# Conditional residual block on one core: LoRA factors and base in SyncE's queue, two packs mixed before the first LoRA product, 24 warm-up matmuls

## The reference

```python
masked_w = weight * mask[None]                                  # (8, 256, 256)
w_bot = einsum('bg,got->bot', cond, masked_w)                   # layer 0's weight per sample
x = x + einsum('bnt,bot->bno', x, w_bot) + bias0
out = einsum('btc,oc->bto', x, W_base) + b_base                 # layer 1's base
h = einsum('btc,erc->bter', x, As)
lora = einsum('bter,eor,be->bto', h, Bs, cond) * 2.0            # rank 16, 8 experts
x = x + out + lora
```

## Time and profile before

| what | us |
|---|---|
| median of 3 runs | 61.73 |
| lowest and highest of them | 61.02 and 61.81 |
| the profiled execution: its own time | 61.96 |
| the profiled execution: its span | 60.0 |

### The profile page before, as it was taken

The page is one execution under the profiler, slowest core; times in us unless marked ns, Lnnn a source line. Parts: engine busy times, 40 slices in busy tenths (PEclk is TensorE's granted clock), DMA queues, the critical chain, the costliest instruction groups (busy, mean ns, idle before and its releaser), DMA issues.

```text
span 60.0 us, 983 instructions
## 1 busy us (share of the span) xinstructions
PE 53.4 (89%) x335; PEld 48.4 (81%) x335; DVE 43.2 (72%) x65; ACT 31.3 (52%) x52; POOL 31.7 (53%) x29
## 2 busy tenths in 40 slices
PE   3926999999999789999978999999999999999910
PEld 3906999999999568898866889989988989888900
DVE  0001983798599699899999999999996974835030
ACT  0805934030760688900299999497099391340700
POOL 4000704403992009999049999999999991000000
PEclk9999999999999999999999999999999999999999
DMA  0889999999999930000026350543140532514472
GB/s 0 138 296 406 404 398 404 407 405 412 412 401 409 401 134 11 0 0 0 0 89 261 116 227 12 186 169 130 51 175 30 205 120 106 206 37 175 175 255 94
DMA packets 5332, 11.79 MB, mean 196 GB/s; under 512 B 592, under 2 KB 1104, under 8 KB 5328
## 3 DMA queue, kind: packets, MB, share of 16 engines
q1 hardware_dynamic: 5040, 11.21, 49.3%
q10 hardware_dynamic: 288, 0.53, 3.0%
HBM read 7.54 MB, written 4.19 MB: 196 GB/s over the span
## 4 chain that ended last, share of the span: by engine, by line
PE 56%; POOL 12%; DVE 9%; issue 9%; DMA 7%; ACT 2%; POOLq 0%; DVEq 0%
PE ps_out L484 9%; PE ps_out L444 9%; PE ps_out L446 9%; PE ps_out L450 9%; DMA packs_sb<-head_dram 7%; PE ps_merge L450 4%; POOL W_lo L195 4%; DVE W L328 4%; POOL W L199 4%; PE ps_merge L446 4%; PE ps_merge L444 4%; PE ps_lora L444 3%; PE ps_lora L446 3%; PE ps_lora L450 3%; POOL W_lo L189 2%
## 5 line engine op out<-in xcount | busy, mean ns | idle before, releaser
L339 DVE TENSOR_TENSOR x_lo<-x_sb,x_hi 128x1024 fp32r<-128x1024 f32 x8 | 12.2, 1530 | 0.0
L189 POOL TENSOR_TENSOR W_lo<-W,W_hi 128x512 fp32r<-128x512 f32 x8 | 10.9, 1359 | 2.4 <-ACT W_hi L232 2.4
L195 POOL TENSOR_TENSOR W_lo<-W,W_hi 128x512 fp32r<-128x512 f32 x6 | 10.1, 1691 | 2.3 <-ACT W_hi L238 2.3
L484 PE MATMUL ps_out<-packs_sb 128*128 128x128 f32 x64 | 9.8, 314 | 1.6 <-DMA packs_sb<-head_dram 1.6
L199 POOL TENSOR_TENSOR W<-W,ident 128x256 f32<-128x256 f32 x6 | 8.5, 1424 | 4.2 <-DVE x_lo L339 4.2
L484 PEld LDWEIGHTS ps_out<-packs_sb 128*128 128x128 f32 x64 | 9.2, 226 | 1.8 <-DMA packs_sb<-head_dram 1.8
L444 PE MATMUL ps_out<-x_hi,M_hi 128*128 128x512 f32 (+1 forms) x32 | 9.9, 390 | 0.3 <-DVE x_lo L339 0.3
L446 PE MATMUL ps_out<-x_lo,M_hi 128*128 128x512 f32 (+1 forms) x32 | 9.7, 384 | 0.0
L450 PE MATMUL ps_out<-x_hi,M_lo 128*128 128x512 f32 (+1 forms) x32 | 9.7, 384 | 0.0
L261 ACT ACTIVATE out_sb<-ps_out,bias_sb 128x512 f32<-128x512 f32 x8 | 5.5, 686 | 7.0 <-DVE bias_sb L419 4.2
L311 DVE SCALAR_TENSOR_TENSOR A_lo<-lora_sb,A_hi 128x256 fp32r<-128x256 f32 x8 | 5.0, 621 | 4.8 <-ACT A_hi L224 4.8
(11 more groups left out here) (49 smaller groups left out, 81.6 us busy)
## 6 DMA issues: line engine op xcount, KB each, us to landing
x_sb<-xT_dram SPq DMA_DIRECT2D x8, 512.0 KB, 10.8
outT_dram<-out_sb SPq DMA_DIRECT2D x15, 256.0 KB, 2.0
packs_sb<-packs_dram SPq DMA_DIRECT2D x7, 288.0 KB, 6.1
rows_sb<-rows_dram SPq DMA_DIRECT2D x1, 384.0 KB, 8.0
lora_sb<-lora_dram ACTq DMA_DIRECT2D x1, 262.0 KB, 4.4
base_sb<-base_dram ACTq DMA_DIRECT2D x1, 256.0 KB, 5.1
outT_dram<-out_sb SPq DMA_DIRECT2D x2, 128.0 KB, 1.8
packs_sb<-head_dram SPq DMA_DIRECT2D x1, 192.0 KB, 4.2
```

The lines of the kernel that those rows point to most:

```text
L189: pool.tensor_tensor(W1_lo[:, b % W1BUF], W1[:, b % W1BUF], W1_hi[:, b % W1BUF].bitcast(f32), ALU.subtract).then_inc(w1lo_done, 1)
L195: pool.tensor_tensor(W0_lo[:, b % 2], W0[:, b], W0_hi[:, b % 2].bitcast(f32), ALU.subtract).then_inc(w0lo_done, 1)
L339: nc.vector.tensor_tensor(x_lo[:, b % XBUF], x_sb[:, b], x_hi[:, b % XBUF].bitcast(f32), ALU.subtract).then_inc(xlo_done, 1)
L484: mm = nc.tensor.matmul(dst[:, j, :, k, :], pack(q)[0][:, k, j * P:(j + 1) * P], mix, start=True, stop=True)
```

## The change

Three things change. The two loads of ScalarE's queue go to SyncE's queue: the LoRA factors stand behind `rest` and ahead of the first full pack, the base behind the second full pack (the third pack of all). On TensorE the second pack is mixed ahead of the first LoRA product, and the third and fourth packs ahead of the second and third LoRA products. The number of warm-up matmuls goes from 21 to 24. VectorE's, GpSimd's and the rest of ScalarE's programs are as before.

```diff
-    WARM = 21
+    WARM = 24
...
             sp.dma_start(packs_sb[:, 0:cut], head).then_inc(mix_in, 16)
             sp.dma_start(packs_sb[:, cut:MIXW + PACKW], rest).then_inc(pack_in[0], 16)
-            for q in range(1, NQ):
+            sp.dma_start(lora_sb[:, :], lora_in).then_inc(lora_arrived, 16)
+            load_pack(1)
+            load_pack(2)
+            sp.dma_start(base_sb[:, :, :], base.rearrange("p (j o) -> p j o", j=NT)).then_inc(base_in, 16)
+            for q in range(3, NQ):
                 load_pack(q)
...
-            act.dma_start(lora_sb[:, :], lora_in).then_inc(lora_arrived, 16)
-            act.dma_start(base_sb[:, :, :], base.rearrange("p (j o) -> p j o", j=NT)).then_inc(base_in, 16)
...
             mixed(0)
+            mixed(1)
             lora(0)
-            mixed(1)
+            mixed(2)
             lora(1)
-            mixed(2)
+            mixed(3)
             lora(2)
-            mixed(3)
             mixed(4)
             lora(3)
```

## The result

| what | before | with the change |
|---|---|---|
| median, us | 61.38 (4 runs) | 62.86 (4 runs) |
| lowest and highest | 60.95 and 61.81 | 62.63 and 63.16 |
| ratio, 95% interval | | 1.0244, 1.0142 to 1.0347 |
| profiled execution: its time and its span | 61.96 and 60.0 | 62.87 and 60.9 |

The change makes the kernel slower by 1.5 us (0.9 to 2.1 by the interval); 62.0 was forecast, in a range of 60.8 to 62.8.

A forecast was written before the change was run, and what follows sets the result against it. The prediction took the end to move with the start of `w0(3)`, behind TensorE's opening and then VectorE; +0.60 for the order, -0.16 and -0.14 for the earlier start gave +0.30 on 61.73, so 62.0 us, range 60.8 to 62.8.

The forecast's parts named there:

- The loads: Opening loads, counted back at 402 GB/s from the third full pack at 8.5 us: `head` 0.3 us earlier, later delays hidden.
- -0.30 for the loads: TensorE's earlier start from `head` landing sooner: -0.16 us for the passes and -0.14 for an earlier change of clock level.
- The second rival: Opening loads: one queue fills slower than two, everything lands 0.53 us later, time 62.4 to 62.6; chance 0.17.
- If the change of level comes as much earlier as the work does: TensorE's clock in the opening: its rise to the high level moves ahead with the work by 0.3 us, worth -0.14 us.
- first rival: TensorE's opening: with more warm-ups and less idle time the full clock comes much sooner, at 7.5 us, giving 60.9; chance 0.20.
- The warm-ups at 0: TensorE before `head`: three more warm-ups end at 3.7 us, ahead of `head` at 4.65, and add 0 on the path.
- The order, +0.60: VectorE before `w0(3)`: `w1(2)` stands ahead and waits for `lora(2)`, moved from pass 42 to 50, so `w0(3)` starts 0.60 us later.
- Delay taken up: VectorE at `w0(3)`: the path doesn't hang on it, so only the earlier start is left, -0.3 us and 61.4; chance 0.13.
- The method's 62.26: The whole kernel: the summed +0.30 us set on the profiled execution of before, 61.96, instead of on the median, 61.73.

The follow-up runs named there:

- g_two: The changed kernel with the same loads spread over SyncE's and ScalarE's queues, TensorE's new order and 24 warm-ups kept; 61.05 us, ratio 1.004 to before.
- e_loads: The kernel before with only the loads of the change, old TensorE order and 21 warm-ups; 62.54 us, ratio 1.024 to before.
- f_hold: The changed kernel with 28 more warm-up matmuls between the first and the second mix; 61.84 us, ratio 1.013 to before.
- h_order36: The kernel before with 36 warm-ups and TensorE's new order, VectorE's order unchanged; 61.06 us, ratio 1.006 to before.
- i_order36_again: The same kernel as h_order36 in ten more executions; 60.88 us, ratio 1.002 to before.
- h_order_dve36: The kernel before with 36 warm-ups, TensorE's new order and VectorE's order made to match; 59.82 us, ratio 0.985 to before.
- g_lora_behind: The changed kernel with the LoRA factors behind the first full pack in SyncE's queue; 62.00 us, ratio 1.022 to before.
- h_loads36: The kernel before with 36 warm-ups and the loads of the change; 61.91 us, ratio 1.018 to before.
- i_hold_dve: The changed kernel with 28 more warm-ups between the first two mixes and VectorE's order made to match TensorE's; 60.58 us, ratio 0.991 to before.

## Why the prediction was wrong

The method held: the end moves as the start of `w0(3)` moves (0.97 and 0.9), and the sum over that stretch was the right one to make. The time lies 0.06 us above the range and 0.86 above the forecast.

*The loads: this is the step that failed.* The prediction took the third full pack to stay at 8.5 and counted back from it at 402 GB/s, into a stretch where the trace showed 212. The count gave `head` 4.65, LoRA 5.7, first full pack 6.45, base 7.8 (its steps redone give 4.6 and 6.4); measured were 3.2, 6.4, 7.15, 8.5. The count was wrong on both sides, and that is worse than a shift: `head` so early let TensorE finish the first mix at 4.8, and the pack so late left it idle for 2.4 us. A pause of TensorE, and the low level behind it, had no term in the sum. `g_two` differs from the changed kernel in the loads alone and takes 1.3 us (by the ratios) to 1.8 us (by the medians) off it, where the sum had -0.30 for the loads; that is nearly all of the loss. `e_loads`, 1.3 us over before, says the same without the new order, which in the prediction's own terms hid 0.5 us of LoRA's delay.

*The second rival* had the mechanism, one queue that fills slower, and its signs (landings 0.5 and more late, decisive when TensorE waits for a pack), with a chance of 0.17. Its price stopped at 62.6, for it left `head` at 4.94 and took one queue to be slower from the start; in fact it was quicker until 3 us and slower until 9. Its argument against itself, DMA engines 0.87 busy, was no argument: with one queue they were 0.82 busy at 136 GB/s. Busy engines there say nothing of how much they move.

*The clock.* "If the change of level comes as much earlier as the work does" took for granted that it rises once. It rose early in the first mix, near 3.8, fell at the pause's end (the granted clock from 7 to 9 us is 0.58: full for 0.3 us, half for the rest), and rose again in `mixed(2)`, near 10.7. The early rise was the first rival's, and passes of the first mix at 0.111 were among the prediction's own signs of being wrong; the rise was worth nothing, since TensorE had no data to use it on. `f_hold` prices the low level behind the pause at 0.7 to 1.0 us.

*The warm-ups at 0* were right as a median (0.997), but the term hid a gain: with 36 the kernel is 1.0 us faster by the ratio and 1.2 by the medians, and its small scatter fits a level that is high early in each of its runs.

*The order, +0.60.* Right in sign, and right that VectorE's program sets it, but at the full clock mis-sized and for a neighbouring reason. The step let `w0(3)` hang on `lora(2)` through `w1(2)`; it hangs on `lora(1)` through `w1(1)`, for VectorE needs 2.4 us for the instructions between, of which the text's 0.6 + 0.4 + 0.6 had left one too short: `a_lo(3)` held VectorE 0.59 us in the changed kernel and 0.78 in `i_order36_again`. At the full clock the order costs 1.1 to 1.3 us (`h_order36` and `i_order36_again`), and `h_order_dve36` takes that away. What it costs in the changed kernel is open between 0 and 0.6 us: `e_loads` without it is as slow by the ratio, but has `w0(3)` 0.6 earlier.

*The Trainium skill's rule* in the prediction (DMA: Bandwidth & Descriptors, "Issuing engines are not separate DMA queues"), that a second issuing engine saves only issue time, differs from what was measured in the opening: 136 to 263 GB/s from 3 to 5 us with one queue, 289 to 370 with two. The measurement decides. From 9 us on the two groups move the same, 401 to 416, and there the rule holds.

*Delay taken up* didn't happen.

*The profiled execution of before.* The method's 62.26 for a profiled execution lies 0.6 under the 62.87 measured, 62.0 lies 0.9 under the median; the smaller gap is no better forecast. The profiled execution of before lies 0.58 above the median of its four runs, where the prediction had 0.23 from the three runs it knew; so 0.35 of the gap on the median comes from before and not from the change.

## What to carry to other kernels

Don't fill the opening of a load stream by counting back at the steady rate; if a small first load is moved ahead, ask how long the engine then waits for the second, and whether its clock survives the pause. When one engine's order is changed, the program of the engine that consumes it has to be changed with it: the same edit cost 1.1 to 1.3 us with the old order on VectorE and 0.1, within 0.4, with a matching one. Warm-up matmuls that reach up to the first data make an early rise of the clock much surer; here 36 for 21 gave 1.6%.

## What the runs showed of the hardware

From 3 to 9 us one queue moved less than two here (the groups overlap a little between 5 and 7), although from 2 to 3 it moved more and its first load landed earlier (`head` at 3.2 against 4.9). The third full pack, with the same bytes ahead of it, landed at 9.2 in the changed kernel and at 7.6 in `g_two`, and one queue in the old places still cost 0.65 us. Why it is slower isn't shown; `g_lora_behind` excludes only that it is LoRA's own load, and with the base issued by 3.5 us a lack of issued loads doesn't explain 136 GB/s from 3 to 5.

TensorE's clock fell to the 1.2 GHz level at about 7.3 us, at the end of a pause of 2.4 us behind a first mix nearly all at the full level. It fell at about 7.5 in `e_loads` (pause from 4.8 to 7.4) and in `h_loads36` (from 5.6 to 7.8), and it rose again at about 10.7 to 10.9 in all three. Behind the 0.64 us of `g_two` and the 0.78 of `g_lora_behind` it didn't fall. And in two single executions it was low to the end: one of `h_order36` took 104.13 us, beside nine of 60.63 to 61.35, and one of `i_hold_dve` 88.42, beside nine of 60.32 to 60.90. The profile of the first has no record of the clock and so reads 1.00, but a product of 256 columns takes 0.22 us from start to start at 67 us and 0.12 in before: that is the 1.2 GHz level. The profile's page of the second has

```profile
PEclk9855555555555555555555555555555555555555
```

There the granted clock is 0.56 from 3.6 us on, between the two levels, and it fell in the midst of work, with no pause of TensorE before it. The same products lie mostly 0.20 us apart, now and then 0.12. Nothing in the two programs explains either, since the others of the same programs ran at full clock; 36 warm-ups don't guard against it, for `h_order36` has them. What sets it off stays open.
